# Three gathers under way in tile 0, later stores and stacks there, and chunk 7 gathered whole from tile 1 on

## What is computed

```
e = stack([tbl_f[ids[:, f]] for f in range(39)], axis=1)
z = einsum('bpc,apc,bpa->bp', e[:, ROW], w, e[:, COL])
h = concatenate([z, dense_ctx], axis=1)
h = maximum(h @ W_top1 + b_top1, 0)
h = maximum(h @ W_top2 + b_top2, 0)
y = h @ W_top3
```

## Time and profile before

| | |
|---|---|
| median of 3 runs | 782.33 us (781.53 to 784.59) |
| profiled execution, its time | 785.84 us |
| its span, first to last instruction | 784.0 us |
| TensorE busy | 714.4 us, 91% |
| VectorE busy | 610.2 us, 78% |
| GpSimd busy (420 gathers) | 409.4 us, 52% |
| ScalarE busy | 104.4 us, 13% |
| DMA, mean rate | 180 GB/s, 141.40 MB |
| granted TensorE clock, mean | 0.970 |

### The profile page before, as it was taken

One profiled execution on the slowest core, in us unless ns is written; L12 is line 12 of the kernel. 1 busy time (PEld: TensorE's weight loads), 2 busy tenths in 40 slices (PEclk: granted clock), 3 DMA queues, 4 the chain that ended last, 5 costly groups with the idle time before them and its releaser, 6 DMA issues.

```text
span 784.0 us, 10892 instructions
## 1 busy us (share of the span) xinstructions
PE 714.4 (91%) x4202; PEld 287.0 (37%) x4202; DVE 610.2 (78%) x773; ACT 104.4 (13%) x186; POOL 409.4 (52%) x424
## 2 busy tenths in 40 slices
PE   1696889897568999999999999999999999999998
PEld 0232233332223444444433444444434434343343
DVE  4665799998556998898878998888869877788640
ACT  3413211110000010101111010110111101011002
POOL 6756434443777755656766555566756566400000
PEclk9789799999788999999999999999999999999999
DMA  7555787579745646364765673547675573543200
GB/s 211 175 178 157 262 268 244 190 244 309 258 147 174 224 124 224 102 202 133 246 227 181 229 225 117 160 131 231 207 243 157 173 243 79 183 163 111 82 1 0
DMA packets 72271, 141.40 MB, mean 180 GB/s; under 512 B 13829, under 2 KB 23704, under 8 KB 72092
## 3 DMA queue, kind: packets, MB, share of 16 engines
q1 hardware_dynamic: 48796, 116.86, 43.4%
q10 hardware_dynamic: 9984, 16.94, 6.2%
q0 software_dynamic: 13440, 6.91, 6.1%
HBM read 109.66 MB, written 31.00 MB: 179 GB/s over the span
## 4 chain that ended last, share of the span: by engine, by line
PE 76%; DVE 7%; issue 6%; POOL 5%; DMA 4%; ACT 2%; SPq 0%; DVEq 0%; ACTq 0%; POOLq 0%
PE z_ps L612 24%; PE u_ps L588 24%; PE t_ps L551 9%; PE m_ps L625 8%; POOL e_rows L416 5%; DVE prod L912 4%; PE m_ps L627 3%; DVE one_hot L900 3%; PE t_ps L532 2%; DMA e_rows<-in_tbl_dram,idx 1%; DMA w<-w_rows 1%; PE u_ps L647 1%; DMA scratch<-parts 1%; PE u_ps L656 1%; PE m_ps L629 1%
## 5 line engine op out<-in xcount | busy, mean ns | idle before, releaser
L912 DVE TENSOR_TENSOR prod<-u_ps,eT 128x1024 f32<-128x1024 f32 x400 | 469.4, 1216 | 113.4 <-PE u_ps L588 112.7
L416 POOL DMA_INDIRECT e_rows<-in_tbl_dram,idx x420 | 409.2, 974 | 270.1 <-DVE prod L912 104.7
L588 PE MATMUL u_ps<-e,w 128*128 128x512 f32 x800 | 255.8, 435 | 16.6 <-DVE prod L912 11.8
L612 PE MATMUL z_ps<-prod,sel 128*32 128x512 f32 x1600 | 262.6, 614 | 0.0
L588 PEld LDWEIGHTS u_ps<-e,w 128*128 128x128 f32 x800 | 134.8, 192 | 160.6 <-DVE prod L912 74.9
L551 PE MATMUL t_ps<-one_hot,tb 125*32 125x512 bf16 x1344 | 134.0, 395 | 12.4 <-DVE one_hot L900 12.0
L900 DVE TENSOR_SCALAR one_hot<-hot_idx,row 125x512 bf16<-125x512 f16 (+2 forms) x296 | 107.7, 421 | 9.3 <-PE t_ps L551 7.3
L612 PEld LDWEIGHTS z_ps<-prod,sel 128*32 128x32 f32 x1600 | 43.5, 108 | 136.6 <-issue 112.6
L551 PEld LDWEIGHTS t_ps<-one_hot,tb 125*32 125x32 bf16 x1344 | 48.4, 99 | 94.8 <-issue 60.4
L625 PE MATMUL m_ps<-zT,w1s 128*128 128x512 f32 x144 | 73.5, 592 | 0.0
L716 ACT CAST parts<-t_ps 128x512 fp32r<-128x512 f32 (+1 forms) x40 | 23.5, 587 | 238.7 <-PE t_ps L551 119.8
(11 more groups left out here) (52 smaller groups left out, 127.2 us busy)
## 6 DMA issues: line engine op xcount, KB each, us to landing
w<-w_rows SPq DMA_DIRECT2D x100, 512.0 KB
e<-scratch SPq DMA_DIRECT2D x62, 512.0 KB, 6.8
scratch<-parts SPq DMA_DIRECT2D x62, 256.0 KB
w_rows<-h ACTq DMA_DIRECT2D x48, 256.0 KB
e_rows<-in_tbl_dram,idx POOLq DMA_INDIRECT x420
hot_idx<-hot SPq DMA_DIRECT2D x12, 512.0 KB, 5.1
h<-in_w_dram ACTq DMA_DIRECT2D x12, 256.0 KB, 4.0
e<-scratch SPq DMA_DIRECT2D x8, 384.0 KB
```

The lines of the kernel that those rows point to most:

```text
L416: pool.indirect_dma_start(e_rows[:, r, n, D * q:D * q + D], None, tables[f], bass.IndirectOffsetOnAxis(ap=idx[:, t, f * TPG + n:f * TPG + ...
L588: last = nc.tensor.matmul(u_ps[:, s % 2, place, :], w4[:, p % WR, (u % PW) * P:(u % PW + 1) * P], e4[:, E4_SLOT[g], j - C * g, :], start=T ...
L612: last = nc.tensor.matmul(z_ps[D * quad:D * quad + D, z % 2, :], sel[:, D - 1 - row:2 * D - 1 - row], prod[:, (NS * t + n) % PR, place, :] ...
L912: nc.vector.tensor_tensor(prod[:, s % PR, :, :], u_ps[:, s % 2, :, :], e, ALU.mult).then_inc(s_mul, 1)
```

## The change

Chunk 7 is looked up in tile 0 only. In tiles 1 to 3 its four fields are gathered: 16 more gathers a tile (124 for 108, 468 for 420 in all), one more turn a tile, and ten slices a tile fewer. The eT buffer of chunk 7 has one place instead of two. In tile 0, three gathers are under way instead of two, the orders of tile 0 and of the other tiles are new, and in tile 0 stores and stacks come later: the stack one batch later up to batch 16; the store one batch later and the stack two batches later for chunks complete in batches 17 to 38.

```
-    return c[1] in HOT_TABLES and (c[1] != 2 or c[0] == 0)
+    return c[1] in HOT_TABLES and (c[1] not in (2, 7) or c[0] == 0)
-GATHERS_PER_TILE = 108
+GATHERS_PER_TILE = 124
-TWO_PLACES = (0, 1, 2, 3, 7)
+TWO_PLACES = (0, 1, 2, 3)
 FIRST_TILE = ((7, 0, None, (0, 0, 0, 1, 1, 1, 2, 2, 2, 2)), (3, 0, 3, ()), (4, 0, 9, ()),
-              (8, 0, None, (10, 10, 11, 11, 12, 12, 13, 13, 14, 14)),
-              (1, 1, None, (15, 16, 16, 17, 17, 18, 18, 19, 19, 20)), (5, 0, 21, ()),
...
+              (8, 0, None, (10, 10, 11, 11, 12, 12, 13, 13, 14, 14)), (5, 0, 19, ()),
+              (1, 1, None, (20, 21, 22, 22, 23, 24, 25, 25, 26, 27)), (6, 0, 28, ()), (9, 0, 31, ()),
+              (2, 1, 40, ()), (0, 1, 43, ()), (3, 1, 48, ()))
-OTHER_TILES = ((8, 0, None, (0, 1, 1, 2, 3, 4, 4, 5, 6, 6)), (4, 0, 7, ()),
...
+OTHER_TILES = ((7, 0, 2, ()), (8, 0, None, (3, 4, 4, 5, 5, 6, 6, 7, 7, 8)), (4, 0, 9, ()), (5, 0, 16, ()),
+               (1, 1, None, (17, 18, 19, 20, 21, 22, 23, 24, 25, 26)), (6, 0, 28, ()), (9, 0, 34, ()),
+               (2, 1, 39, ()), (0, 1, 43, ()), (3, 1, 48, ()))
+LATE = (17, 39)
-WINDOW = 2
+WINDOW = 3
-        STACKS.setdefault(max(b + 2, free), []).append(c)
+
+        late = LATE[0] <= b < LATE[1]
+        STORES.setdefault(b + 1 + late, []).append(c)
+        STACKS.setdefault(max(b + (4 if late else 3 if b < LATE[0] else 2), free), []).append(c)
-                    for c in COMPLETE.get(NBAT * t + b - 1, ()):
-                        if c not in MADE:
-                            store_parts(c)
+                    for c in STORES.get(NBAT * t + b, ()):
+                        store_parts(c)
```

## The result

| | kernel before | changed kernel |
|---|---|---|
| median | 783.46 us, 4 runs (781.53 to 785.94) | 775.17 us, 4 runs (773.39 to 776.26) |
| ratio | | 0.989, 95% interval 0.9851 to 0.9929 |
| profiled execution, its span | 785.84 us, 784.0 | 776.24 us, 774.4 |

The change saves about 8 us in 783 (1.1%), a third of the 27 that I forecast; 775.2 lies above my range of 745 to 770. On another chip, where the kernel before took 787.12, the changed kernel took 774.73 (ratio 0.9863, 0.9797 to 0.9929). In five of the six experiment sessions the kernel before itself took 833 to 867 us, and none of their times can be compared with those here; what they do say is told apart, at the end of the experiments.

A forecast was written before the change was run, and what follows sets the result against it. TensorE, 91% busy, was the engine to follow, held by late gathers in tile 0. Terms -25.8 - 0.4 - 4.7 + 3.8 = -27.1 us took the profiled 785.84 to 758.7, median 755, range 745 to 770.

The forecast's parts named there:

- the stack of chunk 4: Tiles 1 to 3: its landing some 14 us after the turn makes TensorE wait, up to 1.2 us a tile.
- the turn of chunk 7: Tiles 2 and 3, two batches in: last two gathers land in time; 0.5 us a tile for what goes wrong.
- Step 1: Tile 0 gathers: three under way take 125 us for 76 instead of 162, so number 96 could go at 159.
- a third gather would stand behind the others and bring nothing: Rival, tile 0: gather 96 stays at 196, in all +8 us, median 790; chance 0.07.
- Step 2: Tile 0, batch 25: pace by multiplies and landings both allow gather 96 near 160; taken as 161.
- Step 3: End of tile 0: gathers bound it, TensorE waits about 9 us ahead of batch 52's turn; batch 53 comes 25.8 us sooner.
- The weight stall: Tile 0: TensorE's 3.31 us wait for a weight piece at 196 goes, hidden under the wait for gathers.
- the stack of (0, 8): Tile 0, batches 16 to 19: going out one batch later while these batches are shorter costs about 1.5 us.
- Steps 4 to 6: Rest of tile 1, tile 2 and tile 3: -0.4, -4.7 and +3.8 us, -1.3 from batch 53 to the end.
- new waits in tiles 1 to 3: Rival: chunk 7's turn and chunk 4's stack could each cost 3 us a tile, +12, median 767; chance 0.07.
- my case: Whole kernel: likeliest median 755 us, with 748 to 762 given a chance of 0.54.
- The DMA rival: Tile 0: DMA bounds it, weights and stacks come late, (1, 7)'s turn near 250, median 762 to 770; chance 0.2.

The follow-up runs named there:

- w3_3: Kernel before with three gathers under way in tile 0 instead of two and nothing else changed: 766.07 us, ratio 0.9731 to the kernel before.
- lead_3: Changed kernel with gathers from number 96 on let go twelve multiplies (6 batches) earlier: 761.87 us, ratio 0.9682 to the kernel before.
- after_3: Changed kernel run again without edit, as reference for the runs beside it: 774.73 us.
- stacks_3: Changed kernel with stacks one batch earlier up to batch 16, and chunk 8's two batches later from tile 1 on: 764.18 us, ratio 0.9719.

## Why the prediction was wrong

The miss, by the profiled executions, is 776.2 - 758.7 = 17.5 us: 3.4 in tile 0 and 14.1 behind it. The steps that failed are 4 to 6, in two terms of the sum above all: the stack of chunk 4, put at 1.2 us a tile, and the turn of chunk 7, put at 0.5. By my own steps:

**Step 1, three under way: right.** I took 125 us for 76 gathers; 75 took 115.7. The Trainium skill (DMA: Bandwidth & Descriptors, section SWDGE vs HWDGE vs iDMA) states that there is one software queue. What I drew from that, that a third gather would stand behind the others and bring nothing, does not hold here: in w3_3 they came 1.55 us apart for 2.14.

**Step 2, gather 96: "both conditions, landing and pace, come out near 160" was wrong, and the more important half of it.** From 150.1 on only the pace held it, until 163.5. I put it at 161, 2.5 early, and the next 63 took 1.263 us each for 1.25: together the 3.4 that step 3 missed. The size is small. But since I saw two bounds at one place I did not look at the pace as a thing that costs; lead_3 shows that it cost 6.0 us in tile 0 (batch 53 at 240.9 for after_3's 246.9) and, with its waits ahead of batches 102 and 152, 12.9 in all.

**Step 3, the end of tile 0: right in mechanism, -22.4 for -25.8.** The wait ahead of batch 52's turn is there, 4.69 us for "some 9", and 2.36 ahead of batch 48's. lead_3 reaches that turn unhindered at 239.75, where I had 233, so the cover was 5.8 us. The weight stall went, as I said. The wait in batch 19 was too small in my sum: I gave the stack of (0, 8) 1.5 us, and batch 19 took 8.4 (134.1 to 142.6), 4.28 of it idle and the clock down behind.

**Steps 4 to 6, tiles 1 to 3: this is where the prediction fell.** -1.3 predicted, +12.8 measured; tile 1 is 4.0 over its forecast, tile 2 6.2, tile 3 3.9. The two waits were the ones I had named. Two terms were too small and a third was missing:
- The stack of chunk 4, taken at 1.2 a tile "with the stack of (1, 8) just ahead of it". I took 14 us from turn to landing from the earlier trace rows; it was 17.2, with (1, 8)'s 1 MB ahead on the DMA engines. And I left out that the clock falls behind such a wait, as it does in the earlier trace rows. Batches 64 and 65 took 4.9 us more than in stacks_3. stacks_3 takes 5.1 off tile 1 and 3.8 off tile 2 against after_3; in tile 3, where there was no such wait, it takes 1.0 more. That is 7.9 us where I had 3.6.
- The turn of chunk 7, taken at 0.5 for "what goes wrong". It waited 2.23 and 2.83 us; lead_3 takes 5.6 us off tiles 1 to 3 against after_3 where I had 1.0. I counted issue and landing of the last two gathers from the pace and took for granted that GpSimd would be free; in fact it was still sending the ones before, with the least gap of 0.30 us, and number 283 went at 413.18, 4 us after its multiply (the first of batch 100, which ends at 409.2). And the turn came 5.6 us behind its start, where I had counted 2.4 from the turns of tile 0. TensorE was ready at 416.5, so one of the two alone would have cost nothing.
- The first batches of a tile, where the eight `z_ps` matmuls take 1.90 us for 1.07 (411.64 and 296.55, above). Before, slices lay in these batches; now nothing does. Batches 100 and 101 take 3.27 and 2.95 us, where my unit costs give 2.3 each; before they took 8.1 together, where the unit costs give 7.6. By this estimate some 1.1 us was missing from my table in tile 2 and as much in tile 3; in tile 1 these batches lie ahead of batch 53. This has no experiment.

The first two are 8.9 us of the excess by after_3, if they add; the third is some 2, and the rest stays open.

The rival "new waits in tiles 1 to 3" is what happened: +12 by its own sum, 12.8 + 1.3 = 14.1 against my case as measured. I gave it 0.07, and its 767 leaves out the 3.4 us of tile 0. I had named both mechanisms and priced them at their mean path instead of at what stands ahead of them in their queues. The DMA rival did not come: the share between 160 and 196 was 0.83 at 281 GB/s, and no weight stalled. That the changed kernel is faster at all, as I said it would be, it owes to the third gather: by w3_3 that alone gives 21 us, and the rest of the change takes 8.7 of them back.

## What to carry to other kernels

A change that bundles one strong edit with rearrangements should be run with the strong edit alone: here one constant gave 21 us and the whole change 12 beside it. Where work is moved away from in front of a transfer, ask when the transfer lands if nothing else changes: ten slices taken out of batches 15 to 19 became in good part a wait for a stack, and the stretch to batch 28 was only 2.5 us shorter. And the time of a transfer is not its usual one if another megabyte goes out ahead of it; a wait of 3 us on TensorE then costs nearly 5.

## What the hardware showed that I had not expected

A gate by another engine's count can hide behind a wait for landings: it had held nothing at gather 96 in the kernel before, and with the landings faster it cost 13.41 us there. And one program, the kernel before, took 782 to 787 us in some sessions and 833 to 867 in others. It has no trace from the latter; those of its variants show unchanged instruction times and engines that stood for reasons that the trace does not name, and from batch 53 on those with 468 gathers lost 57 to 76 us where those with 420 lost some 30.
